# A GNN layer on Trainium2: each gather of xf fetches 126 rows instead of 125

## The reference

```
h   = gelu(edge_attr @ f_w0 + f_b0)        # 20000 x 50 -> 20000 x 128
h   = gelu(h @ f_w1 + f_b1); h = gelu(h @ f_w2 + f_b2); h = gelu(h @ f_w3 + f_b3)
W   = h * C[:, None]                       # C: cosine cutoff of each edge's length
xf  = x @ lin1_w                           # 1250 x 128
msg = xf[src] * W                          # the gather: one row of xf for every edge
agg = segment_sum(msg, dst, 1250)
out = gelu(agg @ lin2_w + lin2_b) @ lin_w + lin_b
result = layernorm(x + out)
```

## Time and profile before

| | |
|---|---|
| median of 3 runs | 257.4 us |
| profiled execution | 258.03 us |
| its span, first to last instruction | 256.2 us |
| PE, DVE, ACT, POOL busy | 223.5, 135.1, 110.0, 191.1 us |
| share of the span on POOL in the chain that ended last | 53% |
| mean granted TensorE clock | 0.933 |

### The profile page before, as it was taken

One profiled execution on the slowest core, in us unless ns is written; L12 is line 12 of the kernel. 1 busy time (PEld: TensorE's weight loads), 2 busy tenths in 40 slices (PEclk: granted clock), 3 DMA queues, 4 the chain that ended last, 5 costly groups with the idle time before them and its releaser, 6 DMA issues.

```text
span 256.2 us, 3892 instructions
## 1 busy us (share of the span) xinstructions
PE 223.5 (87%) x1130; PEld 148.6 (58%) x1130; DVE 135.1 (53%) x252; ACT 110.0 (43%) x181; POOL 191.1 (75%) x155
## 2 busy tenths in 40 slices
PE   3889999999799999899999599979968997898480
PEld 3535676765666766666766367555626565675350
DVE  5682186553666653666655356644424575613135
ACT  2457655354455364455365334515352453100052
POOL 6887888888888878888877888888778788887000
PEclk9999999999999999999999979989997999955587
DMA  6862222221221221221221212212121211111003
GB/s 209 248 202 72 75 74 46 70 75 46 66 72 42 70 74 41 72 72 41 69 75 41 75 37 72 72 36 72 47 72 40 72 31 43 41 45 45 10 0 101
DMA packets 17904, 17.70 MB, mean 69 GB/s; under 512 B 9244, under 2 KB 15183, under 8 KB 17894
## 3 DMA queue, kind: packets, MB, share of 16 engines
q0 software_dynamic: 11296, 9.52, 15.4%
q1 hardware_dynamic: 5872, 7.48, 9.6%
q10 hardware_dynamic: 726, 0.59, 0.8%
HBM read 16.14 MB, written 1.28 MB: 68 GB/s over the span
## 4 chain that ended last, share of the span: by engine, by line
POOL 53%; PE 21%; issue 15%; DVE 3%; ACT 2%; DMA 1%; POOLq 1%; ACTq 1%; another core or an unknown queue 1%; DVEq 1%
POOL gathered L310 53%; PE ps_agg L483 3%; PE ps_even L470 3%; PE ps_even L457 2%; PE ps_even L448 2%; PE ps_odd L457 2%; PE ps_even L462 2%; PE ps_odd L462 2%; PE ps_pick L509 1%; PE ps_odd L470 1%; DMA gathered<-xf_dram,src_idx 1%; PE ps_even L576 1%; DVE stats L762 1%; PE ps_odd L576 1%
## 5 line engine op out<-in xcount | busy, mean ns | idle before, releaser
L310 POOL DMA_INDIRECT gathered<-xf_dram,src_idx x138 | 180.4, 1307 | 42.1 <-issue 41.1
L483 PEld LDWEIGHTS ps_agg<-onehot,messages 125*128 125x128 f32 x320 | 43.8, 204 | 38.8 <-DVE messages L682 22.2
L483 PE MATMUL ps_agg<-onehot,messages 125*128 125x64 f32 x320 | 45.0, 287 | 17.8 <-DVE messages L682 15.9
L337 ACT ACTIVATE h<-ps_odd,biases_sb 128x500 f32<-128x500 f32 x61 | 41.3, 677 | 34.0 <-PE ps_odd L462 14.4
L337 ACT ACTIVATE h<-ps_even,biases_sb 128x500 f32<-128x500 f32 x61 | 40.9, 670 | 21.4 <-PE ps_even L462 9.7
L335 ACT ACTIVATE h<-pre 125x512 f32<-125x512 f32 x40 | 25.0, 626 | 51.8 <-DVE pre L666 43.4
L682 DVE TENSOR_TENSOR messages<-h,gathered 125x512 f32<-125x512 f32 x38 | 26.1, 690 | 32.5 <-DMA gathered<-xf_dram,src_idx 30.7
L470 PEld LDWEIGHTS ps_odd<-w_mlp_sb,h 128*125 128x125 f32 x160 | 21.3, 194 | 9.8 <-issue 9.8
L509 PE MATMUL ps_pick<-xf_parts,pick 128*125 128x384 bf16 x140 | 25.7, 331 | 0.0
L666 DVE TENSOR_TENSOR pre<-ps_odd,row_b_sb 125x512 f32<-125x512 f32 x20 | 13.8, 692 | 22.4 <-PE ps_odd L470 17.9
L509 PEld LDWEIGHTS ps_pick<-xf_parts,pick 128*125 128x125 bf16 x140 | 18.0, 136 | 12.5 <-issue 9.6
(11 more groups left out here) (107 smaller groups left out, 184.5 us busy)
## 6 DMA issues: line engine op xcount, KB each, us to landing
edge_in<-in_edge_attrT SPq DMA_DIRECT2D x44, 97.7 KB
gathered<-xf_dram,src_idx POOLq DMA_INDIRECT x138
picked_i<-in_picked_src SPq DMA_DIRECT2D x1, 875.0 KB
xf_dram<-xf_sb SPq DMA_DIRECT2D x2, 256.0 KB
lin_xT_sb<-in_lin_xT SPq DMA_DIRECT2D x1, 369.0 KB
lin_xT_sb<-in_lin_xT SPq DMA_DIRECT2D x1, 320.0 KB, 3.1
w_mlp_sb<-in_w_mlp ACTq DMA_DIRECT2D x1, 256.0 KB
out<-normed SPq DMA_DIRECT2D x1, 256.0 KB
```

What stands on the lines that cost most here:

```text
L310: nc.gpsimd.indirect_dma_start(out=gathered[0:TILE, b, t, :], out_offset=None, in_=xf_dram[:, :], in_offset=bass.IndirectOffsetOnAxis(ap=s ...
L337: nc.scalar.activation(out_ap, in_ap, GELU, bias=biases_sb[:, layer:layer + 1]).then_inc(done, 1)
L483: last = nc.tensor.matmul(ps_agg[:, b * WINDOW:(b + 1) * WINDOW], messages[:, slot, t, :], onehot[:, p % 2, b * TILES_PER_GROUP + t, :], s ...
```

## The change

The indirect DMA at L310 gets 126 indices and writes 126 partitions. Row 125 of `gathered`, which was never written before, receives row 0 of xf (its index is 0); nothing reads it, since the messages still read partitions 0 to 124. The 138 gathers, their order, their waits and their semaphores stay, and so does every instruction of the other engines. The eight gathers of x at L294 are not touched.

```diff
@@ -17,6 +17,7 @@
 PAIR_TILES = 2 * TILES_PER_GROUP
 ROWS = 128
+GATHER_ROWS = 126
 NODE_CHUNKS = -(-NODES // ROWS)
@@ -308,8 +309,8 @@
                         nc.gpsimd.indirect_dma_start(
-                            out=gathered[0:TILE, b, t, :], out_offset=None, in_=xf_dram[:, :],
-                            in_offset=bass.IndirectOffsetOnAxis(ap=src_idx[0:TILE, tile:tile + 1], axis=0),
+                            out=gathered[0:GATHER_ROWS, b, t, :], out_offset=None, in_=xf_dram[:, :],
+                            in_offset=bass.IndirectOffsetOnAxis(ap=src_idx[0:GATHER_ROWS, tile:tile + 1], axis=0),
                         ).then_inc(gather_landed[b], 16)
```

## The result

| | before | 126 rows |
|---|---|---|
| median, us | 257.95 (257.32 to 261.54, 4 runs) | 296.94 (295.76 to 300.17, 4 runs) |
| ratio to before | | 1.154 (95%: 1.142 to 1.166) |
| profiled execution / its span | 258.03 / 256.2 | 300.17 / 298.3 |
| mean granted TensorE clock | 0.933 | 0.868 |

A forecast was written before the change was run, and what follows sets the result against it. GpSimd's gather issuing was taken to bound the kernel from 134 us on, PE before. From 258.03 us, 27.8 us off up to the last scatter and 0.7 us off the tail gave 229.5 us, range 226.5 to 240.

The forecast's parts named there:

- Bound now: Whole kernel: PE sets the pace up to 134 us, then GpSimd's issuing of gathers, 1.61 us each, sets the end.
- Price of a gather: Gather L310: falls from 1.203 to 0.965 us by entries per engine, saving GpSimd 32.8 us over 138 gathers.
- rival by packets: Gather L310: price goes by packets per engine, 1.03 us, giving 233.8 us; chance 0.14.
- nothing changes: Gather L310: price stays at 1.20 or 1.21 us, giving 258 to 259.4 us; chance 0.07.
- slower rival: Gather L310: 126 rows cut into fewer shares than 125, giving 293 us with 3, 336 with 2; chance 0.06.
- So what is late next is PE: From pair 13 at 138.73 us: PE, undisturbed, reaches the epilogue's add at 203.1 instead of 219.45 us, 16.3 us saved.
- Up to 134 us, PE as before: First part of the kernel: the new profile should show PE's work unchanged until 134 us.
- No wait for a slot: GpSimd's gather slots: freed at some 44 us, reached at about 54 us for group 10, so no wait expected.
- Epilogue and tail: After the epilogue's add: last scatter ends at 214.1 instead of 241.9 us; faster node products save another 0.7 us.
- The forecast of 1.00 for the clock: TensorE: granted clock stays at 1.00 until the node stage.

The follow-up runs named there:

- e10: Kernel before (125 rows), with TensorE's picking product for the last tile of every pair above 0, so five gathers fewer (133): 251.9 us, ratio 0.977.
- e7: Changed kernel (126 rows) with gathered rows 64 bytes wide instead of 512, same gathers and shares: 301.0 us.
- e4: Changed kernel (126 rows) with GpSimd at most four groups ahead of the messages instead of eight: 280.2 us, ratio 1.081 to the kernel before.
- e13: Changed kernel (126 rows) with eight small memsets behind each gather, period 1.545 us: 259.6 us, ratio 1.006 to the kernel before.
- e8: Kernel before (125 rows) with eight more small SyncE loads per pair into memory that nothing reads: 259.3 us, ratio 1.002.
- e12: Changed kernel (126 rows) with six memsets behind each gather and picking products in every pair above 0 (133 gathers): 247.7 us, ratio 0.958 to the kernel before.
- e11: Changed kernel (126 rows) with six memsets behind each gather, period 1.475 us: 254.6 us, ratio 0.983 to the kernel before.
- e6: Changed kernel with 119 rows a gather instead of 126 (7 shares of 17 rows), the left-out rows zeroed: 264.0 us (246.8 to 274.7).
- e5: Changed kernel (126 rows) with four memsets behind each gather, period 1.446 us: 261.3 us (252.6 to 266.4).

## Why the prediction was wrong

- *Bound now.* Right. e10 confirms that GpSimd's issuing sets the end of the kernel before.
- *Price of a gather.* Right: 0.988 us at the median for 0.965 forecast, 0.968 at the shortest, gaps of 0.30 us kept, 48 packets. It goes by the rows of one engine, as I took it (e7). The Trainium skill's page "DMA: Bandwidth & Descriptors", section "Why a DMA increments its semaphore by 16 and not by 1", has the transfer run on the largest number of engines up to 16 that divides the slowest dimension, which is 14 for 126 rows; the 48 packets agree. The rival by packets (1.03 us) fell, and so did "nothing changes". The slower rival, fewer shares (0.06), had the right sign by the wrong mechanism.
- *"So what is late next is PE", at 8.28, 9.70, 9.70 and 9.83 us a pair.* This step failed. I took the pace of TensorE and the engines behind it as given, whatever GpSimd does, because they wait for nothing of GpSimd's but the gathers. They do depend on it: when gathers follow each other every 1.29 us, TensorE's semaphore counts get out late, and VectorE, ScalarE and SyncE stand still with their inputs done. It already fails in the first 60 us, where I had written "Up to 134 us, PE as before".
- *No wait for a slot.* Wrong as a consequence: with messages late the slots stay full, 53.0 us of waits, and during these pauses more than half of the late counts come through (41 of 73).
- *Epilogue and tail.* Never tested, as the run never came to that state. The forecast of 1.00 for the clock fell with the stalls.
- *What was there to see.* The kernel before had one wait of 1.5 us for "remote" and 1% for an unknown queue in its chain, on one core, where nothing unknown should be. 9% of TensorE's counts were late already, all in two stretches around pairs without a picking product. I read past it. A faster engine was asked about only as a supplier of data, not as a load on what others use.

Shown: the counts of TensorE alone are late, in order, while gathers run; the delay builds up in an unbroken run (e4); on the whole it falls with a longer period, and it is gone at 1.545 us with the same split (e13); the bytes (e7) and completions in another queue (e8) don't make it. Shown too, and not seen in the prediction: the period of the gathers is only one side. With the same form and period of gathers, a picking product in every pair above 0 took the counts over 0.3 us late from 9% to none (e10 against before) and from 28% to none (e12 against e11), in one trace each. Why is open. A pair without this product takes TensorE 8.28 us and not 9.70, so its counts follow each other faster there. Or the counts get through while a gather is held up: in the kernel before, VectorE built a pick matrix from 66.01 us on, and the gather at 66.27 took 2.25 us instead of 1.20. Against the second: in e10 no gather took over 1.4 us between those starting at 38.2 and 57.1 us, and nothing was late. No run separates the two.

Not excluded: a part of the number of engines. e6 with 7 engines has fewer late counts than e5 with 14 at a longer period, and no kernel with 5 engines was run below 1.503 us. Argued only: that the writes with which GpSimd issues a gather share a way with TensorE's counts. If so, it isn't their mass: the kernel before wrote 80 packets a gather, 53 per us, and the changed one 48, 37 per us, with far more late. No run here reaches inside that. Open too is why e6 scatters by 28 us.

## What to carry to other kernels

Before an issuing engine is made faster, read the waits whose releaser the profile can't name; on one core they may be counts that come late, and here a higher rate of issue made them worse. Aim at the rate that the consumer needs and not at the cheapest form: 138 gathers at 1.475 us (254.6 us, though one of four runs took 261.9) beat the same at 1.29 us (296.9 us) and, by less, at 1.545 us (259.6 us). Fewer DMAs (e10, 0.977) relieved the engine here without any late count, and let the faster gathers of e11 keep their gain (e12, 0.958).

## What the runs showed of the hardware that I had not expected

- TensorE's semaphore counts, and only they, are held back while GpSimd issues indirect DMAs back to back: 40% over 0.3 us late at a period of 1.291 us, up to 20 us, and none at 1.545 us. They come out in order; in the burst at 57.4 us the recorded ones are 0.04 to 0.10 us apart.
- The period isn't all: at 1.475 us 28% of the counts are late with 14 picking products on TensorE, and at 1.478 us none with 19.
- The cost of issuing an indirect DMA goes by the rows of one share, not by all rows, bytes or packets (e7): 128 rows (8 each) 0.944 us, 126 (9 each) 0.988, 100 (10 each) 1.003, 119 (17 each) 1.093, 125 (25 each) 1.203.
- Small memsets behind an indirect DMA cost less than their length: two of 0.17 us in all made the period 0.06 us longer, as the gap before the next gather shrank from 0.30 to 0.18 us.
